# Causal attention on one core: the mask added in VectorE's maximum pass, softmax sums added on GpSimd before one ones product

## The reference, cut to what matters

```python
scores = einsum('bhsd,bhtd->bhst', qh, kh) * scale
mask = triu(ones((Sq, Sq), bool), k=0).at[0, 0].set(False)
scores = where(mask, -inf, scores)
probs = softmax(scores, axis=-1)
out = einsum('bhst,bhtd->bhsd', probs, vh)
x = x + out @ Wo.T + bo
```

## Time and profile before

| | us |
|---|---|
| median of 3 runs | 2806.88 (2805.59 to 2806.93) |
| profiled execution, span (first to last instruction) | 2803.6 |
| a steady batch, from S unit 0 to S unit 0 of the next (754.19 to 853.97) | 99.8 |
| PE, DVE, ACT, POOL busy in 754 to 854 | 96.1, 69.0, 39.5, 19.7 |
| feed-forward loop, PE busy of 1043 us | 1035.7 |

### The profile page before, as it was taken

How to read it: one execution, slowest core, us unless ns; L and a number is a source line. 1 busy time by engine, 2 the same in 40 slices (tenths; PEclk the granted TensorE clock), 3 DMA queues, 4 the chain that set the end, 5 groups by cost and what they waited for, 6 DMA issues and landing times. The chain is left out here.

```text
span 2803.6 us, 46166 instructions
## 1 busy us (share of the span) xinstructions
PE 2666.3 (95%) x15410; PEld 1979.3 (71%) x15410; DVE 1688.5 (60%) x3278; ACT 1111.7 (40%) x1965; POOL 377.6 (13%) x791
## 2 busy tenths in 40 slices
PE   7999999999999999999999967999999999999998
PEld 5666666667666666666766645888888888888887
DVE  4676766776767677677676666444444444444444
ACT  2533443443353344244335245444344334433332
POOL 1212121121121212112112110000000000000000
PEclk9999999999999999999999977999999999999999
DMA  4343253333334325333333332000000000000000
GB/s 129 84 112 99 61 135 92 81 98 98 88 85 114 97 62 134 90 79 103 98 85 88 96 104 76 30 30 30 30 30 30 30 30 30 30 30 30 30 30 31
DMA packets 116803, 198.81 MB, mean 71 GB/s; under 512 B 19987, under 2 KB 22035, under 8 KB 116260
## 3 DMA queue, kind: packets, MB, share of 16 engines
q1 hardware_dynamic: 116772, 198.42, 25.6%
HBM read 63.08 MB, written 33.55 MB: 34 GB/s over the span
## 5 line engine op out<-in xcount | busy, mean ns | idle before, releaser
L715 ACT ACTIVATE probs<-bank 128x512 f32<-128x512 f32 x640 | 369.2, 597 | 339.6 <-PE bank L529 329.6
L1125 PE MATMUL y_bank<-projT,a_hi 128*128 128x512 f32 x1024 | 409.1, 399 | 0.0
L1113 PE MATMUL h_bank<-x2T_hi,fcT 128*128 128x512 f32 x1024 | 406.2, 397 | 0.9 <-ACT scale_row L1196 0.9
L1114 PE MATMUL h_bank<-x2T_lo,fcT 128*128 128x512 f32 x1024 | 406.6, 397 | 0.0
L1127 PE MATMUL y_bank<-projT,a_lo 128*128 128x512 f32 x1024 | 403.9, 394 | 0.0
L1204 ACT ACTIVATE relu<-h_bank,scale_fc 128x512 f32<-128x512 f32 x256 | 176.0, 687 | 464.8 <-PE h_bank L1117 464.8
L464 POOL TENSOR_SCALAR_AFFINE_SELECT probs<-probs 128x256 f32<-128x256 f32 (+1 forms) x640 | 234.1, 366 | 872.7 <-ACT probs L715 870.1
L1314 DVE CAST a_hi<-act_sq 128x512 fp32r<-128x512 f32 x256 | 121.0, 472 | 373.6 <-ACT act_sq L1209 373.6
L529 PE MATMUL bank<-stack 98*128 98x512 f32 (+3 forms) x1024 | 286.0, 351 | 28.3 <-ACT probs L715 26.0
L504 PE MATMUL bank<-stack 96*128 96x512 f32 (+3 forms) x1024 | 266.0, 330 | 17.8 <-DVE maxima L777 11.8
L777 DVE TENSOR_REDUCE maxima<-bank 128x1 f32<-128x512 f32 x256 | 175.9, 687 | 162.2 <-PE bank L508 162.2
(11 more groups left out here) (182 smaller groups left out, 4623.9 us busy)
## 6 DMA issues: line engine op xcount, KB each, us to landing
stack<-stage SPq DMA_DIRECT2D x768, 128.0 KB, 2.3
x_in<-in_x_dram SPq DMA_DIRECT2D x16, 1024.0 KB, 5.3
x<-x_res SPq DMA_DIRECT2D x64, 256.0 KB, 2.4
x_in_sb<-x SPq DMA_DIRECT2D x16, 1024.0 KB, 5.6
out_dram<-y_sb SPq DMA_DIRECT2D x64, 256.0 KB, 2.0
xc_rows<-in_ctx_dram SPq DMA_DIRECT2D x15, 1024.0 KB, 5.2
stack<-m_stage SPq DMA_DIRECT2D x128, 8.0 KB, 1.8
w_nat<-in_L_ffn_w_fc_dram SPq DMA_DIRECT2D x2, 1024.0 KB, 6.7
```

The source lines that it names most:

```text
L715: act.activation(probs[:, s[2], :], t_bank[u % 2][:, :], ACT.Exp, scale=SCALE).then_inc(exp_done, 1)
L1113: pe.matmul(h_bank[b % 2][:, :], fcT[:, k, cols], xT_hi[:, k, :], start=k == 0, stop=False)
L1114: pe.matmul(h_bank[b % 2][:, :], fcT[:, k, cols], xT_lo[:, k, :], start=False, stop=False)
L1125: pe.matmul(y_bank[j][:, :], a_hi[:, b % RING, P * j:P * j + P], projT[:, b, :], start=b == 0, stop=False)
```

## The change

Four things are done, all in `attention_phase`.

1. The 40 mask products of a batch go. VectorE's reduction becomes `tensor_tensor_reduce`: add a bf16 mask tile, write the sum back to the bank, and keep the maximum. A unit of 256+256 is now two such calls. 
2. For groups 0 to 2 the 16 ones products go. GpSimd adds the key blocks of each head into `acc` after each five selected units (`add_pair`), and a new step ONES, behind NC, does one ones product of 512 columns for each head. Group 3 keeps its old products.
3. Sums are turned by VectorE's 32x32 transpose (NT), so that 16 columns hold them all, reciprocals are taken of 128x16 (NR), and a second transpose spreads them (NB). ScalarE no longer copies the sum bank, and makes the high part (NH) in all groups.
4. The buffer `x_in` goes. x is loaded into `xc_rows` and normalized there; the residual is loaded a second time into `x_res`, by a transfer at the head of the batch.

```diff
-        return [("NR", g, c) for c in range(4)] + [("NM", g, 0), ("NH", g, 0), ("NL", g, 0)]
+        return [("NT", g), ("NR", g), ("NB", g), ("NM", g, 0), ("NH", g, 0), ("NL", g, 0)]
...
-        return score("T", g, 0, at) + [("NC", g - 1)] + score("T", g, at)
+        return score("T", g, 0, at) + [("NC", g - 1), ("ONES", g - 1)] + score("T", g, at)
...
+                    elif s[0] == "XRES":
+                        wait_alone(sp, sp_passed, (mm_free, first), (x2_stored, START + i * 16 * TT))
+                        sp.dma_start(x_res[:, :, :], x[bass.ds(i, 1)].rearrange("a (j p) d -> p (a j) d", p=P)
+                                     ).then_inc(res_loaded, 16)
                     elif s[0] == "X_LOAD":
-                        wait_alone(sp, sp_passed, (xres_ready, i * TT + TT))
-                        sp.dma_start(x_in[:, :, :], x[bass.ds(i + 1, 1)]...
+                        wait_alone(sp, sp_passed, (mm_full, first))
+                        sp.dma_start(xc_rows[:, :, :], x[bass.ds(i + 1, 1)]...
...
+            def add_pair(chain, g, pair, i):
+                heads = (2 * pair, 2 * pair + 1)
+                pool.wait_ge(selected, i * TB + UNITS * g + 5 * pair + 5)
+                pool.wait_ge(ones_done, START + i * (GROUPS - 1) + g)
+                for h in heads:
+                    (u0, _), (u1, _) = unit_of(h, 0), unit_of(h, 1)
+                    chain.inc(pool.tensor_tensor(acc[:, h, P:S], probs[:, u0, P:S], probs[:, u1, 0:S - P], ALU.add))
+                for h in heads:
+                    chain.inc(pool.tensor_copy(acc[:, h, 0:P], probs[:, unit_of(h, 0)[0], 0:P]))
+                pool.wait_ge(acc_step, chain.now() - 2)
+                for h in heads:
+                    u2, cols = unit_of(h, 2)
+                    chain.inc(pool.tensor_tensor(acc[:, h, 2 * P:S], acc[:, h, 2 * P:S],
+                                                 probs[:, u2, cols:cols + S - 2 * P], ALU.add))
+                for h in heads:
+                    u3, cols = unit_of(h, 3)
+                    pool.wait_ge(acc_step, chain.now() - 1)
+                    last = pool.tensor_tensor(acc[:, h, 3 * P:S], acc[:, h, 3 * P:S],
+                                              probs[:, u3, cols:cols + P], ALU.add)
...
+                        if k % 5 == 4 and s[1] < GROUPS - 1:
+                            add_pair(chain, s[1], k // 5, i)
...
-                    return mask(out[:, 384:512], masks[:, 0, :])
+                    return block(2 * pair + u // 2, 3, 0)
...
-                for target in (o_bank, sum_bank):
+                for target in (o_bank, sum_bank) if g == GROUPS - 1 else (o_bank,):
...
+                    elif s[0] == "ONES":
+                        g = s[1]
+                        pe.wait_ge(acc_ready, i * 2 * (GROUPS - 1) + 2 * g + 2)
+                        pe.wait_ge(sums_read, START + i * GROUPS + g)
+                        for h in range(GH):
+                            last = pe.matmul(sum_bank[HD * h:HD * h + HD, :], ones[:, 0:HD], acc[:, h, :],
+                                             start=True, stop=True)
+                        last.then_inc(ones_done, 1)
...
+                        if s[1] > 0 and s[2] % 5 == 0:
+                            act.wait_ge(acc_ready, i * 2 * (GROUPS - 1) + 2 * (s[1] - 1) + s[2] // 5 + 1)
...
+                            return dve.tensor_tensor_reduce(
+                                out=bank_u[:, cols:cols + t1], in0=bank_u[:, cols:cols + t1], in1=added, scale=1.0,
+                                scalar=LOWEST, op0=ALU.add, op1=ALU.max,
+                                accum_out=maxima[:, 4 * h + r:4 * h + r + 1])
...
+                        dve.transpose(o_recip[:, :], sum_bank[:, :]).then_inc(sums_read, 1)
...
+                        chain.inc(dve.reciprocal(o_small[:, :],
+                                                 o_recip[:, :].rearrange("p (b c) -> p b c", c=32)[:, :, 0]))
...
+                        chain.inc(dve.transpose(o_recip[:, :].rearrange("p (b c) -> p b c", c=32),
+                                                o_small[:, :].unsqueeze(2).broadcast_to([P, S // 32, 32])))
```

More of the change, by code:

```diff
@@ L26 @@
 MASKED = -1e30
+LOWEST = -3.0e38
 UNITS = 10
@@ L114, in batch_steps @@
     steps += score("T", 3, 0, 4) + weave(score("T", 3, 4), [("OA", j, g) for j in range(2) for g in range(2)])
[L115 to L119, removed]
+    steps += [("NC", 2), ("ONES", 2)] + [("OA", j, g) for j in range(2, 4) for g in range(2)] + norm(2)[:4]
+    steps += pv(3)[:1] + nxt(("CT", 0)) + pv(3)[1:2] + nxt(("CT", 1)) + norm(2)[4:] + pv(3)[2:]
+    steps += [("NT", 3), ("NR", 3), ("NB", 3), ("NM", 3, 0), ("NH", 3, 0), ("NM", 3, 1), ("NL", 3, 0), ("NH", 3, 1),
+              ("NM", 3, 2), ("NL", 3, 1)]
     steps += nxt(("K", 0), *stack(0))
-    steps += [("NH", 3, 2), ("NL", 3, 2), ("NR", 3, 3), ("NM", 3, 3), ("NH", 3, 3), ("NL", 3, 3)]
+    steps += [("NH", 3, 2), ("NL", 3, 2), ("NM", 3, 3), ("NH", 3, 3), ("NL", 3, 3)]
     steps += [("OC", j) for j in range(4)] + [("OB", j) for j in range(4)]
@@ L267, in attention_phase @@
         ident = sb("ident", [P, P])
-        ident_bf = sb("ident_bf", [P, P], BF16)
-        masks = sb("masks", [P, 3, P], BF16)
+        causal = sb("causal", [P, S], BF16)
+        causal_first = sb("causal_first", [P, P], BF16)
+        o_small = sb("o_small", [P, S // 32])
         ones = sb("ones", [P, P])
@@ L467, in select, with unit_of @@
                                           channel_multiplier=-(P + 1) if first_block else -1)
+            def unit_of(h, r):
+                base = 5 * (h // 2)
+                return {0: (base + 2 * (h % 2), 0), 1: (base + 2 * (h % 2) + 1, 0),
+                        3: (base + 2 * (h % 2) + 1, 384), 2: (base + 4, 256 * (h % 2))}[r]
+            def add_pair(chain, g, pair, i):
[17 more added lines that the diff above has]
+                                              probs[:, u3, cols:cols + P], ALU.add)
+                    if h == heads[0]:
+                        chain.inc(last)
+                last.then_inc(acc_ready, 1)
@@ L469, in program @@
             def program(steps, i, first, parity):
+                chain = None if i is None else Tally(acc_step, i * (GROUPS - 1) * 14)
                 for s, n, _ in jobs(steps, first, parity):
                     if s[0] == "XRES":
-                        pool.wait_ge(x_loaded, i * 16 + 16)
+                        pool.wait_ge(res_loaded, i * 16 + 16)
                         pool.wait_ge(mm_free, first)
-                        pool.wait_ge(x2_stored, START + i * 16 * TT)
                         for j in range(TT):
-                            pool.tensor_tensor(x_res[:, j, :], x_in[:, j, :], bias_sb[:, :], ALU.add
+                            pool.tensor_tensor(x_res[:, j, :], x_res[:, j, :], bias_sb[:, :], ALU.add
@@ L483, in program @@
                         select(view, k % 5 in (0, 2)).then_inc(selected, 1)
+                        if k % 5 == 4 and s[1] < GROUPS - 1:
+                            add_pair(chain, s[1], k // 5, i)
+                if i is not None:
+                    assert chain.local == 14 * (GROUPS - 1)
             in_loop(pool, program)
```

111 lines of the change are left out of this document (57 added, 54 removed).

## The result

The changed kernel takes 2880.27 us (median of 4 runs, 2873.24 to 2886.33) against 2806.9 (4 runs, 2805.59 to 2810.53): ratio 1.026, 95% interval 1.024 to 1.028. The forecast was 2835 with a range of 2768 to 2888: slower, as forecast, but by 73 us and not by 28. The profiled execution has a span of 2884.6 us, 81.0 above the 2803.6 of before.

The account below looks back on a forecast made before the run. TensorE, busy 96.1 of 100 us, was the busiest engine, with three chains ending within a microsecond of it. Sections +0.2 and clock +1.9 give +2.1 in 15 batches, +31, last batch -3: span 2832, median 2835 us, range 2768 to 2888.

Parts of the forecast that it names:

- What TensorE is given: Masks (4.4) and sums (6.6) leave TensorE, ONES adds 2.85: 8.1 us a batch less, mostly turned into waits.
- VectorE: Maxima passes: each second instruction costs 0.1 us (bounds 0.075 and 0.25), adding 1.7 us to each group's maxima.
- Rival C: VectorE becomes the bound at 0.25 us for each second instruction: about 7 us a batch, 2915 us; chance 14%.
- GpSimd: Additions with copies take about 5.0 us a pair (4.4 to 6.0), six pairs 30 us a batch, between the selects.
- Sections, without falls: One steady batch, stretch by stretch, minus is gained: -0.3 - 0.5 + 0 + 0.3 + 0 + 0.8 - 0.1 = +0.2 us.
- PV and S of group 2: PV of group 0: 0 kept, standstill 3.2 us. S of group 2: M 0.8 us late, copies decide, +0.3.
- The clock: Standstills bring clock falls: +1.3 us at the layernorm, +0.6 together near 805 and 823, in each of 15 batches.
- The copies of the stack: S of group 0 to S of group 1: six copies, issued by SP in 3.80 us, decide; only -0.3 us kept.
- The last batch: It has no layernorm behind PV of group 0, so it keeps about 3 us of gain.
- What would show it: Signs: TensorE stands over 3 us after V3, PV of group 2 waits 2 us or more, GpSimd near 50 per 100.
- Rival A: No falls of the clock; waits as forecast: 15 x 0.2 - 3 = 0, 2807 us; chance 13%.
- Rival B: Faster: VectorE's second instruction hides behind the pass, GpSimd takes 4.4 us a pair; -1.8 us a batch, 2777 us; chance 27%.

Follow-up runs that it names:

- mask_only: The kernel before with only the mask moved into VectorE's maximum pass (40 mask products a batch fewer): 2804.26 us, ratio 0.9997.
- fill_0: The changed kernel with filler products of the sums' shape put back behind P*V of group 0 alone (2.2 us a batch): 2840.99 us, ratio 1.0134.
- ones_early_only: after_filled with the ones product of group 0 moved from behind the 6th to before the 3rd T unit of group 1: 2798.98 us, ratio 0.9980.
- sums_only: The changed kernel with the mask put back as 40 products a batch on TensorE; new sums and column reciprocals stay: 2886.89 us, ratio 1.0294.
- after_filled: The changed kernel with products that compute nothing in five standstills of TensorE, about 5.5 us a batch: 2818.51 us, ratio 1.0049.
- no_adds: The changed kernel without GpSimd's additions and the waits for them; the ones product still runs, on a constant array: 2869.17 us, ratio 1.0233.

## Why the prediction came out as it did

- *What TensorE is given.* The work did leave: the page counts 13618 products instead of 15410, 112 a batch fewer. No run measures the 8.1 us by themselves. The statement that a busy share of 96% must not be booked as gain was right.
- *VectorE.* Its second instruction is there 64 times a batch and lasts 141 ns, but starts together with the next pass; successive passes of 512 and 384 columns start 0.61 and 0.52 us apart (818.09, 818.70, 819.22 in the changed kernel), so it costs 0.01 us for 512 columns, 0.06 for 384 and 0.04 for 128 (0.61, 0.52 and 0.24 against 0.60, 0.46 and 0.20 before), below my lower bound of 0.075. My 1.7 us a group were too much: mask_only has BN-M2 unchanged and T2-M3 0.53 longer. Rival C fell: 63.9 us busy, not over 85 (its own sum, 15 x 7.1 - 3, gives 2910 and not 2915). The trace of the changed kernel has 1024 of these passes and 1024 reads of the accumulator, one behind each pass.
- *GpSimd.* Additions of 384, 256 and 128 columns take 1.01, 0.80 and 0.49 us, copies 0.33: 5.3 a pair by the means, 5.0 forecast. GpSimd is busy 44.9 us in 100, 50 forecast. The six additions of a pair are 4.6 of its 5.3 us.
- *Sections, without falls.* S of groups 0 and 1, with the norm of group 3: -0.9 forecast, -0.25 and -0.62 measured. PV and S of group 2: +0.3 against +0.98 and -0.39 (with fill_0's 19.02). S of group 3: 0 against +1.23 and -1.20. ONES of group 2: +0.8 against +1.03. In all +0.2 forecast, +0.8 measured. Half of the miss is in group 2. I had its step M 0.8 us late, mostly by VectorE's 1.7; it is 0.98 late, and the cause is the ones product of group 0: mask_only has the new passes and no delay, and ones_early_only takes 0.95 back by moving the product. The copies behind M give back 0.39 and not 0.5. Most of the rest is the ones product of group 2.
- *The clock: the step that failed.* "+1.3 at the first place" and "at the other two, every second batch, with slack behind the first of them: +0.6 together" make 1.9 us a batch. Measured as the mean above the smallest, BN-M2 has 1.9, T2-M3 0.5, M3-T3 1.0 and T3-PV3 0.9, together 4.3, less the 0.5 that before has in T3-PV3: 3.8. At the first place the falls came in 14 of 14 turns, as forecast, but a single one costs 1.6 us there and not 1.3, and in four turns two came in a row. At the second place they came in 9 of 14 turns (in one of them two), at the third in all 14 (in three of them two), not in half. There is slack behind the second place, as I wrote: where one fall lies in T2-M3, the stretch is 0.6 to 0.9 us longer, of 1.7 us of clock lost. Behind the third there is little, 1.3 to 1.6 us lost by each, and that one place costs 1.4 us a turn above before, where I had 0.6 for both. The 3 us at half speed that the sum uses are 3.4 us at a granted clock of 0.50 in the traces, in the changed kernel as in the four falls of the kernel before (in the one of rows 9 the clock is 0.79, 0.50, 0.50 and 0.51 in the microseconds from 229 to 233). The direction of this step was right, and its size half.
- *The copies of the stack.* I kept them in S of group 1 as decided by SP's pace. In 4 of the 14 turns TensorE waits 1.2 to 1.9 us there, in the others 0.3 to 0.6 (the turn from 926.63, then that from 1032.13):

```profile
1016.38 0.73 PE L540 MATMUL bank<-stack 96*128 96x512 f32 x3 [1.36 <-DMA stack<-stage]
```

```profile
1120.61 0.72 PE L540 MATMUL bank<-stack 96*128 96x512 f32 x3 [0.41 <-DMA stack<-stage]
```

  Before never waits over 0.4 for them. With other small delays from PV3 on it is 0.5 us a turn that I had not in the sum. The second load of x runs in the same DMA queue just before (issued at 1006.81 us, 5.8 us to landing by the median; the copies follow from 1009.67), but is not enough to cause it: sums_only has that load and never waits over 0.4 in its 14 turns. mask_only has no such load, and waits for the copies twice in every turn, up to 0.77 us. In their 14 turns, waits over 0.6 stand only in kernels whose masks are in VectorE's pass, where the S units in front are shorter for TensorE. What makes them 1.9 us in single turns stays open.
- *The last batch.* -3 forecast, +9.7 measured; the falls there were not counted. It has no transposes or layernorm for a next batch to fill in, so TensorE stood 3.29 us for the copy of the maxima, and the clock stayed at the lower level for 20 us (the rows show length, busy time of each engine, clock and DMA):

```profile
1682.22 2.36 PE L577 MATMUL bank<-probs,v_sb 128*32 128x512 f32 x32
1687.88 1.22 PE L557 MATMUL bank<-stack 98*128 98x512 f32 x3 [3.29 <-DMA stack<-m_stage]
```

```profile
1687.00:1700.00 13.00, 11.88 (x39) 8.53 (x40) 7.42 (x29) 5.60 (x10) 6.08 (x13) 0.50 0.27 62
1700.00:1707.50 7.50, 5.67 (x37) 2.03 (x36) 5.08 (x11) 1.64 (x4) 7.42 (x15) 0.51 0.01 3
```

  In after_filled this batch takes 169.4 us, 0.5 less than before.
- *What would show it.* Standstill 2.88 us where over 3 was announced; P*V of group 2 waits 1.15 for a select where 2 was (and that wait is hidden). Rival A (no falls) gave 2807; after_filled, which has none in its turns, measured 2818. Rival B has half of its machinery right (the second instruction all but hidden; the pair takes 5.3 us and not 4.4) and its sum wrong.

Against the forecast on the span (+28): 14 turns x 0.6 = 8 us from the sections, 14 x 1.9 = 27 from falls, 14 x 0.5 = 7 from the waits for the copies and the small delays, 12.7 from the last batch, and -2 because 14 turns, not 15, lie between the layernorms: 53, the difference between 81 and 28.

## What to carry to other kernels

Work taken from TensorE in front of a chain of fixed length is not only no gain: it lengthens a standstill, and here the longer standstills brought 3.4 us at half clock behind them in every turn. Before such a change, list each place the work leaves, what is waited for there, and what the clock does behind; put real work (as the ones product and the Q part) or products that compute nothing into the standstill. And judge such an edit with the filler in place, since here 62 of 73 us came back with 5.5 us a batch of useless products.

## What the runs showed of the hardware beside this

- VectorE and GpSimd slowed each other in the changed kernel: VectorE's product of two tiles in SBUF, 512 columns (o_norm by o_recip), takes 965 ns there, 692 in no_adds and 689 before; the low part of cT 882, 691 and 693. By single instructions of the changed kernel's turns, the product takes 691 ns where no instruction of GpSimd runs beside it and 936 to 1232 where its additions or copies into `acc` do; and GpSimd's additions of 256 columns take 951 ns beside one of VectorE's two-tile passes and 729 otherwise. First the changed kernel, then no_adds, 84 to 1500 us:

```profile
L867 DVE TENSOR_TENSOR o_norm<-o_norm,o_recip 128x512 f32<-128x512 f32 x41 | 39.6, 965 | 2.7
```

```profile
L861 DVE TENSOR_TENSOR o_norm<-o_norm,o_recip 128x512 f32<-128x512 f32 x42 | 29.1, 692 | 2.7
```

- In the 14 turns of the changed kernel every fall lasted 3.4 us at a granted clock of 0.50, or 6.8 where two came in a row. A standstill of 0.45 and one of 0.20 us in sparse T units brought falls in 4 of 14 turns of the kernel before, and closing these two ended them all.
